# A grouped matrix product with residual: one x tile asked for ahead of a weight load, and the second half of the second weights prepared by three engines

## The chip, the cores and the metric

The kernel runs on 1 core of one Trainium2 chip. The metric is the device time in microseconds (us) of that core; the time of a kernel is the median of its runs. Within the core the engines named here are PE (TensorE, matmuls), PEld (its weight loads), DVE (VectorE), ACT (ScalarE), POOL (GpSimd) and SP (SyncE, which only issues transfers).

## The reference

There are 128 batches, each a 128 x 512 tile of x, and 32 classes, each with a 512 x 512 weight matrix and a bias row. Every batch has a class id from 0 to 30:

```python
selected_W = W[ids]                    # x: (128, 128, 512), W: (32, 512, 512)
selected_b = b[ids]
out = x + einsum('bti,bio->bto', x, selected_W) + selected_b[:, None, :]
```

Everything is float32. In the drawn ids class 0 has 6 batches, class 1 has 3, class 2 has 9 and class 3 has 4.

## The kernel before, in words

**The computation.** The residual is folded into the weights: 1 is added to the diagonal of every weight matrix, so out = x (W + I) + b. A product at float32 accuracy is made of three products of a faster format (fp32r): each operand is split into a high part (a rounded copy) and a low part (the operand less its high part). Per batch PE runs 4 row blocks x 3 pairs (high x with high W, high x with low W, low x with high W) = 12 matmuls of 128 x 128 by 128 x 512, all into one PSUM tile pA (four of them, used in turn). The batches are run in the order of their classes, so that the weights of each class are loaded once. The first instructions compute that order from the ids.

**The x tiles.** SP asks for tile i of x (function x_load, line 171; helper load, line 196) into one of 8 buffers xs. ACT (high, lines 308 to 317) writes the high part xh (line 314) and then a copy of x into PSUM, pT (line 317). DVE (low, line 372) writes the low part xl from pT and xh (line 375). For the first tile, and for the first weights, DVE subtracts from SBUF directly (lines 379 and 384). When a batch is done, DVE adds the bias to pA and writes os (line 411), and SP stores it (line 222). In DVE's program order low(i + 2) stands ahead of the addition of batch i. xh and xl have 4 buffers, pT has 3.

**The weights.** The first weights (class 0) are prepared in pieces by DVE (add_one, line 339: diagonal; low_w, line 384: low part) and ACT (high_w, line 306: high part). The second weights (class 1) come as two halves of 512 KB (w1_load, line 179, W1 = row blocks 0 and 1, then 2 and 3). POOL prepares each half alone: diagonal (line 255, tensor_tensor), high part wh (line 257, tensor_scalar), low part wl (line 259, tensor_tensor). Then it waits for a bias row, announces class 1 by s_w, asks for the next bias rows and the weights of class 3, and goes on with class 2 and all the others (lines 265 to 291), each with the same three steps on the whole matrix.

**The order around the change.** SP's queue is written out by hand (lines 205 to 217): x tile 1, first half of the second weights, x tiles 2 and 3, bias row 0, second half, x tile 4, the third weights, x tile 5, bias row 1, then the loop in which load(i + 6) stands ahead of the store of batch i. A batch on PE waits for its class's weights (s_w), for the addition of the batch four before (s_fin), for xh (s_xh) and, ahead of its low-x products, for xl (s_xl). Batches 1 to 5 run their high-x products first, later batches the low-x products first. Batch 0 is special: it is run from the pieces of the first weights (lines 477 and 488). The matmuls of all other batches are line 461.

Of the kernel before, what the change touches and what calls it, by code (L numbers as in the profile page):

```python
# [5 lines left out]
def cond_resid(nc, xt, ids, W, bias, out):  # L6
# [5 lines left out]
    f32 = mybir.dt.float32  # L12
# [3 lines left out]
    ALU = mybir.AluOpType  # L16
    ACT = mybir.ActivationFunctionType
    AX = mybir.AxisListType

    B, D = 128, 512  # L20
# [7 lines left out]
    NH = 4  # L28
# [3 lines left out]
    LA = 2  # L32
# [12 lines left out]
    with ExitStack() as ctx:  # L45
# [3 lines left out]
        def sem(name):  # L49
            return ctx.enter_context(nc.semaphore(name))  # L50
# [55 lines left out]
        s_b0 = [sem(f"s_b0{i}") for i in range(2)]  # L106
        s_bb = [sem(f"s_bb{i}") for i in range(C // NB)]
        s_wh = sem("s_wh")
        s_w = sem("s_w")
        s_raw = sem("s_raw")  # L110
        s_xb = sem("s_xb")
# [20 lines left out]
        def chunk(c, k0, k1):  # L132
            return slice(slot(c) + k0 * D, slot(c) + k1 * D)

        def raw(c, k0, k1):
            return wr[:, c % NR, k0 * D:k1 * D]

        def diagonal(c, k0, k1):

            t = wr[:, c % NR, k0 * D + k0 * 128:]  # L140
            return bass.AP(t.tensor, t.offset, [list(t.ap[0]), [D + 128, k1 - k0], [1, 128]])

        def ones_on(n):

            t = ident[:, :]
            return bass.AP(t.tensor, t.offset, [list(t.ap[0]), [0, n], [1, 128]])
# [27 lines left out]
        @block.sync  # L174
        def _(eng):
            eng.dma_start(idr[:, :], ids.rearrange("(a n) -> a n", a=1)).then_inc(s_id, 16)
            def w1_load(h):
                k0, k1 = W1[h]
                eng.dma_start(raw(1, k0, k1), stored(1, k0, k1)).then_inc(s_w1[h], 16)  # L179

            first = [eng.alloc_register(f"first{i}") for i in range(8)]
            lead = eng.alloc_register("lead")

            def sorted_first(i):
                return eng.snap(first[i], min_val=EXP, max_val=EXP + (C + 1) * B - 1) % B  # L185

            eng.wait_ge(s_t0, 1)
            eng.load(lead, best[:, :].bitcast(i32))  # L188
            x_load(eng, 0, bass.ds(eng.snap(lead, min_val=BITS, max_val=BITS + (C + 1) * B - 1) % B, 1))  # L189
            eng.dma_start(raw(0, 3, KT), stored(0, 3, KT)).then_inc(s_w0[2], 16)  # L190
            eng.wait_ge(s_t0, 2)
            eng.load(first, top[0:1, :])  # L192
            ahead = table(eng, "la", tbc, B, 0, B - 1)
            behind = table(eng, "st", tbc, B, 0, B - 1)

            def load(i):
                b = sorted_first(i) if i < 8 else ahead(i)
                if i == NX:
                    eng.wait_ge(s_xb, 2 * len(REST))
                    eng.wait_ge(s_mm, 2)  # L200
                elif i > NX:
                    eng.wait_ge(s_pt, i - NX)
                x_load(eng, i, bass.ds(b, 1))

            load(1)
            w1_load(0)
            load(2)
            load(3)
            bias_load(eng, 0, 1, s_b0[0])
            w1_load(1)  # L210
            load(4)
            eng.wait_ge(s_wd, KT)
            eng.wait_ge(s_raw, 1)
            eng.dma_start(wr[:, 0, :], stored(2, 0, KT)).then_inc(s_w2, 16)
            load(5)
            bias_load(eng, 1, 2, s_b0[1])
            eng.wait_ge(s_tab, 1)
            for i in range(B):
                if i + AHEAD < B:
                    load(i + AHEAD)  # L220
                b = behind(i)
                eng.dma_start(out[bass.ds(b, 1), :, :].rearrange("a t d -> (a t) d"), os[:, i % NO, :])\
                   ._wait_ge(s_fin, i + 1).then_inc(s_o[i % NO], 16)

        @block.gpsimd
        def _(eng):
            eng.iota(rev[:, :], [[1, 128]], base=C * B, channel_multiplier=0,
                     allow_small_or_imprecise_dtypes=True).then_inc(s_io, 1)
            eng.iota(iot[:, :], [[1, 128]], base=0, channel_multiplier=0,
                     allow_small_or_imprecise_dtypes=True).then_inc(s_io, 1)  # L230
            eng.memset(ident[:, :], 0.0).then_inc(s_cst, 1)
            eng.wait_ge(s_cst, 1)
            eng.affine_select(out=ident[:, :], in_=ident[:, :], compare_op=ALU.not_equal, fill=1.0,
                              base=0, pattern=[[-1, 128]], channel_multiplier=1).then_inc(s_cst, 1)
            eng.iota(dif[:, :], [[1, 128]], base=0, channel_multiplier=-1,
                     allow_small_or_imprecise_dtypes=True).then_inc(s_io, 1)
            eng.iota(num[:, 0:1], [[1, 1]], base=0, channel_multiplier=1,
                     allow_small_or_imprecise_dtypes=True).then_inc(s_io, 1)
            eng.iota(thr[:, :], [[B, C]], base=B, channel_multiplier=0,
                     allow_small_or_imprecise_dtypes=True).then_inc(s_io, 1)  # L240
            def load(c):
                eng.dma_start(wr[:, c % NR, :], stored(c, 0, KT)).then_inc(s_wr[c % NR], 16)  # L242
                if c % NB == 0:
                    bias_load(eng, c, c + NB, s_bb[c // NB])

            eng.sem_inc(s_w, 1)
            eng.wait_ge(s_cst, 2)
            done = table(eng, "dn", tn[2:3, :], C, 1, B + 1)
            eng.wait_ge(s_wd, KT)
            for h, (k0, k1) in enumerate(W1):  # L250
                half = raw(1, k0, k1)
                at = chunk(1, k0, k1)
                eye = diagonal(1, k0, k1)
                eng.wait_ge(s_w1[h], 16)
                eng.tensor_tensor(eye, eye, ones_on(k1 - k0), ALU.add).then_inc(s_ri, 1)  # L255
                eng.wait_ge(s_ri, 1 + h)
                eng.tensor_scalar(wh[:, at], half, 1.0, 1.0, ALU.mult, ALU.mult).then_inc(s_wh, 1)  # L257
                eng.wait_ge(s_wh, 1 + h)
                eng.tensor_tensor(wl[:, at], half, wh[:, at].bitcast(f32), ALU.subtract).then_inc(s_wp, 1)  # L259
            eng.wait_ge(s_wp, 2)  # L260
            eng.wait_ge(s_b0[1], 16)
            eng.sem_inc(s_w, 1)
            bias_load(eng, 2, NB, s_bb[0])
            load(3)
            for c in range(2, C):
                if c == 2:
                    eng.wait_ge(s_w2, 16)
                else:
                    eng.wait_ge(s_wr[c % NR], 16 * ((c - 1) // NR))
                eye = diagonal(c, 0, KT)  # L270
                eng.tensor_tensor(eye, eye, ones_on(KT), ALU.add).then_inc(s_ri, 1)  # L271
                at = chunk(c, 0, KT)
                if c == NW:
                    eng.wait_ge(s_tab, 3)
                if c >= NW:
                    n = done(c - NW)
                    eng.wait_ge(s_mm, n).then_inc(s_free, 1)
                eng.wait_ge(s_ri, 1 + c)
                eng.tensor_scalar(wh[:, at], wr[:, c % NR, :], 1.0, 1.0, ALU.mult, ALU.mult).then_inc(s_wh, 1)  # L279
                eng.wait_ge(s_wh, c + 1)  # L280
                if c % NB == 0:
                    eng.wait_ge(s_bb[c // NB], 16)
                eng.tensor_tensor(wl[:, at], wr[:, c % NR, :], wh[:, at].bitcast(f32),  # L283
                                  ALU.subtract).then_inc(s_wp if c == 2 else s_w, 1)
                if c == 2:
                    eng.wait_ge(s_wp, 3)
                    eng.wait_ge(s_bb[0], 16)
                    eng.sem_inc(s_w, 1)
                if c + NR < C:
                    eng.wait_ge(s_w, c + 1)  # L290
                    load(c + NR)

        @block.scalar
        def _(eng):
# [33 lines left out]
                high_0(ks, s_xb)  # L328
            for i in range(2, B):
                high(i)  # L330
        @block.vector
        def _(eng):
            n = [0]
# [66 lines left out]
            eng.tensor_scalar(tn[:, :], pS[0:3, B:B + C], 1.0, None, ALU.add).then_inc(s_tab, 1)  # L400
            eng.wait_ge(s_tab, 3)
            row = table(eng, "bo", tv[1:2, :], B, 0, (C - 1) * D)
            for i in range(B):
                if i + LA < B:
                    low(i + LA)
                at = row(i)
                if i == 0:
                    eng.wait_ge(s_b0[0], 16)
                if i >= NO:
                    eng.wait_ge(s_o[i % NO], 16 * (i // NO))  # L410
                eng.tensor_tensor(os[:, i % NO, :], pA[i % NA][:, :], bb[:, bass.ds(at, D)],  # L411
                                  ALU.add)._wait_ge(s_mm, i + 2).then_inc(s_fin, 1)
# [126 lines left out]
```

## Time and profile before

| | us |
|---|---|
| median of 3 runs | 359.7 |
| the 3 runs | 359.15, 359.70, 359.71 |
| the profiled execution, own time | 359.8 |
| its span in the trace | 358.5 |
| PE busy | 354.6 (99%) |
| DVE, ACT, POOL busy | 172.4, 146.8, 266.8 |

The span runs from the first to the last instruction that the profiler recorded; 1.3 us of the execution's own time lie around it. The granted TensorE clock is at full speed in all 40 slices of the page. Busy time says which engine has the most work; where a microsecond is lost is seen in the chain of waits and in the order of time.

### The profile page before, as it was taken

What the parts mean: (1) busy time and instruction counts of PE and PEld (TensorE: products, weight loads), DVE (VectorE), ACT (ScalarE), POOL (GpSimd) and SP (SyncE); (2) the same over time, 40 slices, a digit from 0 to 9 for tenths busy, and PEclk for the clock granted to TensorE, in tenths of its full rate; (3) what the DMA queues carried; (4) which work ended last, traced back from release to release, by engine and by line L of the source; (5) the groups of instructions that cost most, each with busy time, mean ns of one, the idle gap of its engine ahead of it and who ended that gap; (6) DMA issues with size and microseconds to landing.
All of it is one profiled execution on the core that took longest, in us unless ns stands there. A gap on an engine that the chain in (4) does not pass through costs nothing.

```text
span 358.5 us, 6658 instructions
## 1 busy us (share of the span) xinstructions
PE 354.6 (99%) x1554; PEld 290.2 (81%) x1554; DVE 172.4 (48%) x282; ACT 146.8 (41%) x263; POOL 266.8 (74%) x144
## 2 busy tenths in 40 slices
PE   9999999999999999999999999999999999999996
PEld 4788888888888888888888888888888888888885
DVE  7555355545544544554454454445445445544542
ACT  4564254434433443343443344344334253534420
POOL 1699999997747698799964999799979799935000
PEclk9999999999999999999999999999999999999999
DMA  7999998999886999889998899989998998856622
GB/s 225 375 311 406 413 348 314 324 375 358 280 313 242 354 317 309 295 297 359 338 306 291 283 388 314 341 290 371 317 331 272 358 379 298 327 207 194 191 105 100
DMA packets 43380, 109.49 MB, mean 305 GB/s; under 512 B 4817, under 2 KB 4818, under 8 KB 38610
## 3 DMA queue, kind: packets, MB, share of 16 engines
q1 hardware_dynamic: 37730, 70.01, 54.8%
q0 software_dynamic: 5328, 38.28, 30.8%
q10 hardware_dynamic: 288, 0.79, 0.6%
q8 instruction: 17, 0.28, 0.3%
q14 instruction: 17, 0.14, 0.1%
HBM read 75.50 MB, written 33.55 MB: 304 GB/s over the span
## 4 chain that ended last, share of the span: by engine, by line
PE 96%; DMA 2%; SPq 1%; DVE 0%; issue 0%; ACT 0%
PE pA L461 96%; DMA xs<-xt 2%; DMA idr<-ids 0%; SPq L171 0%; DVE os L411 0%; ACT xh L314 0%; SPq L192 0%; SPq L179 0%; SPq L190 0%; DVE top L354 0%; DVE key L351 0%; SPq L185 0%; SPq L188 0%; SPq L189 0%; DVE best L351 0%
## 5 line engine op out<-in xcount | busy, mean ns | idle before, releaser
L411 DVE TENSOR_TENSOR os<-pA,bb 128x512 f32<-128x512 f32 x128 | 88.5, 691 | 165.3 <-PE pA L461 164.7
L314 ACT ACTIVATE xh<-xs 128x512 fp32r<-128x512 f32 x126 | 79.7, 633 | 194.6 <-PE pA L461 108.4
L283 POOL TENSOR_TENSOR wl<-wr,wh 128x2048 fp32r<-128x2048 f32 x30 | 138.7, 4623 | 2.5
L461 PE MATMUL pA<-wh,xh 128*128 x508 | 135.9, 389 | 0.3 <-ACT xh L314 0.3
L461 PE MATMUL pA<-wl,xh 128*128 x508 | 135.8, 389 | 0.0
L461 PE MATMUL pA<-wh,xl 128*128 x508 | 135.6, 389 | 0.0
L461 PEld LDWEIGHTS pA<-wh,xh 128*128 128x128 f32 x508 | 95.3, 188 | 20.4 <-ACT xh L314 0.7
L461 PEld LDWEIGHTS pA<-wl,xh 128*128 128x128 f32 x508 | 95.4, 188 | 19.8
L461 PEld LDWEIGHTS pA<-wh,xl 128*128 128x128 f32 x508 | 95.4, 188 | 19.7
L375 DVE TENSOR_TENSOR xl<-pT,xh 128x512 fp32r<-128x512 f32 x127 | 86.6, 682 | 16.2 <-ACT pT L317 15.3
L279 POOL TENSOR_SCALAR wh<-wr 128x2048 fp32r<-128x2048 f32 x30 | 57.5, 1918 | 37.3 <-PE pA L461 35.4
L317 ACT ACTIVATE pT<-xs 128x512 f32<-128x512 f32 x126 | 73.5, 583 | 0.0
L271 POOL TENSOR_TENSOR wr<-wr,ident 128x512 f32<-128x512 f32 x30 | 39.2, 1307 | 1.0 <-DMA wr<-w 0.3
L242 POOL DMA_DIRECT2D wr<-w x29 | 17.1, 588 | 8.6 <-POOL wl L283 8.0
L255 POOL TENSOR_TENSOR wr<-wr,ident 128x256 f32<-128x256 f32 x2 | 1.5, 737 | 9.1 <-DMA wr<-w 9.1
L418 PE MATMUL pA<-const-bfloat16-1.0 128*128 128x512 bf16 (+1 forms) x16 | 5.1, 486 | 0.8 <-PEq L532 0.8
L150 POOL DMA_DIRECT2D bb<-bias x8 | 4.5, 559 | 0.7 <-POOL wl L259 0.7
L259 POOL TENSOR_TENSOR wl<-wr,wh 128x1024 fp32r<-128x1024 f32 x2 | 4.8, 2410 | 0.2
L418 PEld LDWEIGHTS pA<-const-bfloat16-1.0 128*128 128x128 bf16 x16 | 1.7, 134 | 2.7 <-issue 2.4
L306 ACT ACTIVATE wh<-wr 128x512 fp32r<-128x512 f32 x4 | 2.3, 618 | 2.1 <-DVE wr L339 2.1
L384 DVE TENSOR_TENSOR wl<-wr,wh 128x512 fp32r<-128x512 f32 x4 | 2.7, 689 | 0.2
L257 POOL TENSOR_SCALAR wh<-wr 128x1024 fp32r<-128x1024 f32 x2 | 2.1, 1050 | 0.2
(51 smaller groups left out, 19.4 us busy)
## 6 DMA issues: line engine op xcount, KB each, us to landing
xs<-xt SPq DMA_DIRECT2D x128, 256.0 KB, 5.8
out<-os SPq DMA_DIRECT2D x128, 256.0 KB, 5.2
wr<-w POOLq DMA_DIRECT2D x29, 1024.0 KB, 7.7
bb<-bias POOLq DMA_DIRECT2D x7, 1024.0 KB, 10.4
wr<-w SPq DMA_DIRECT2D x2, 512.0 KB, 6.8
wr<-w SPq DMA_DIRECT2D x1, 1024.0 KB, 8.6
wr<-w ACTq DMA_DIRECT2D x1, 512.0 KB, 3.3
bb<-bias SPq DMA_DIRECT2D x2, 256.0 KB, 7.8
```

The costliest lines, as they stand in the source:

```text
L150: eng.dma_start(bb[:, at].rearrange("p (c d) -> p c d", c=j1 - j0), bias[j0:j1, :].rearrange("(a c) d -> a c d", a=1).to_broadcast([128, j ...
L242: eng.dma_start(wr[:, c % NR, :], stored(c, 0, KT)).then_inc(s_wr[c % NR], 16)
L259: eng.tensor_tensor(wl[:, at], half, wh[:, at].bitcast(f32), ALU.subtract).then_inc(s_wp, 1)
L271: eng.tensor_tensor(eye, eye, ones_on(KT), ALU.add).then_inc(s_ri, 1)
L279: eng.tensor_scalar(wh[:, at], wr[:, c % NR, :], 1.0, 1.0, ALU.mult, ALU.mult).then_inc(s_wh, 1)
L283: eng.tensor_tensor(wl[:, at], wr[:, c % NR, :], wh[:, at].bitcast(f32), ALU.subtract).then_inc(s_wp if c == 2 else s_w, 1)
L314: eng.activation(xh[:, i % NH, :, :], xs[:, i % NX, :, :], ACT.Copy).then_inc(s_xh, 1)
L317: eng.activation(pT[i % NT][:, :, :], xs[:, i % NX, :, :], ACT.Copy).then_inc(s_pt, 1)
L375: eng.tensor_tensor(xl[:, i % NH, :, :], pT[i % NT][:, :, :], xh[:, i % NH, :, :].bitcast(f32), ALU.subtract).then_inc(s_xl, 1)
L411: eng.tensor_tensor(os[:, i % NO, :], pA[i % NA][:, :], bb[:, bass.ds(at, D)], ALU.add)._wait_ge(s_mm, i + 2).then_inc(s_fin, 1)
L418: eng.matmul(pA[0][:, 0:w], fill[:, 0:128], fill[:, 0:w], start=True, stop=True)
L461: mm = eng.matmul(pA[i % NA][:, :], xp[:, i % NH, k, :], wp[:, bass.ds(at + k * D, D)], start=(n == 0), stop=(n == 3 * KT - 1))
```

## The change

Three things. On SP's queue the request for x tile 2 stands ahead of the first half of the second weights. For the second half of the second weights DVE adds the diagonal (signal s_rb), ACT writes the high part (signal s_hb) and POOL writes only the low part. ACT's instruction stands behind high(3), and waits there for s_rb. On DVE the low parts of x tiles 2 and 3 are written first, then DVE waits for the half to land and adds the diagonal, and only then comes the loop with the additions of the bias (in it the low parts from tile 4 on). In POOL's loop over the later classes two waited counts are one smaller, since POOL itself counts one diagonal and one high part fewer.

```diff
-            w1_load(0)
             load(2)
+            w1_load(0)
             load(3)
             bias_load(eng, 0, 1, s_b0[0])
             w1_load(1)
...
-            for h, (k0, k1) in enumerate(W1):
-                half = raw(1, k0, k1)
-                at = chunk(1, k0, k1)
-                eye = diagonal(1, k0, k1)
-                eng.wait_ge(s_w1[h], 16)
-                eng.tensor_tensor(eye, eye, ones_on(k1 - k0), ALU.add).then_inc(s_ri, 1)
-                eng.wait_ge(s_ri, 1 + h)
-                eng.tensor_scalar(wh[:, at], half, 1.0, 1.0, ALU.mult, ALU.mult).then_inc(s_wh, 1)
-                eng.wait_ge(s_wh, 1 + h)
-                eng.tensor_tensor(wl[:, at], half, wh[:, at].bitcast(f32), ALU.subtract).then_inc(s_wp, 1)
+            eye = diagonal(1, *W1[0])
+            eng.wait_ge(s_w1[0], 16)
+            eng.tensor_tensor(eye, eye, ones_on(W1[0][1]), ALU.add).then_inc(s_ri, 1)
+            eng.wait_ge(s_ri, 1)
+            eng.tensor_scalar(wh[:, chunk(1, *W1[0])], raw(1, *W1[0]), 1.0, 1.0, ALU.mult, ALU.mult).then_inc(s_wh, 1)
+            eng.wait_ge(s_wh, 1)
+            for h in range(2):
+                at = chunk(1, *W1[h])
+                if h == 1:
+                    eng.wait_ge(s_hb, 1)
+                eng.tensor_tensor(wl[:, at], raw(1, *W1[h]), wh[:, at].bitcast(f32), ALU.subtract).then_inc(s_wp, 1)
...
-                eng.wait_ge(s_ri, 1 + c)
+                eng.wait_ge(s_ri, c)
...
-                eng.wait_ge(s_wh, c + 1)
+                eng.wait_ge(s_wh, c)
...
             for i in range(2, B):
                 high(i)
+                if i == NH - 1:
+                    eng.wait_ge(s_rb, 1)
+                    eng.activation(wh[:, chunk(1, *W1[1])], raw(1, *W1[1]), ACT.Copy).then_inc(s_hb, 1)
...
+            for i in range(LA, NH):
+                low(i)
+            eye = diagonal(1, *W1[1])
+            eng.wait_ge(s_w1[1], 16)
+            eng.tensor_tensor(eye, eye, ones_on(2), ALU.add).then_inc(s_rb, 1)
             for i in range(B):
-                if i + LA < B:
+                if NH <= i + LA < B:
                     low(i + LA)
```

## Rows read from the trace of the kernel before

**Rows 1.** The page: the chain that ended last, by line; and one group.

```profile
PE pA L461 96%; DMA xs<-xt 2%; DMA idr<-ids 0%; SPq L171 0%; DVE os L411 0%; ACT xh L314 0%; SPq L192 0%; SPq L179 0%; SPq L190 0%; DVE top L354 0%; DVE key L351 0%; SPq L185 0%; SPq L188 0%; SPq L189 0%; DVE best L351 0%
...
L375 DVE TENSOR_TENSOR xl<-pT,xh 128x512 fp32r<-128x512 f32 x127 | 86.6, 682 | 16.2 <-ACT pT L317 15.3
```

**Rows 2.** Chain that ended last, in order of time: start us, us, what.

```profile
5.79 6.20 DMA xs<-xt
...
12.01 0.64 ACT xh L314
...
12.69 343.03 PE pA L461 x1512
```

**Rows 3.** Timeline of PE: start us, us, instruction [idle before <-releaser].

```profile
9.50 1.07 PE L461 MATMUL pA<-wh,xh 128*128 x4
...
15.55 1.07 PE L461 MATMUL pA<-wh,xh 128*128 x4
...
20.99 1.07 PE L461 MATMUL pA<-wh,xh 128*128 x4
...
354.64 1.07 PE L461 MATMUL pA<-wh,xh 128*128 x4
```

**Rows 4.** Timeline of SP's queue, same columns; L171 x tiles, L179 second weights.

```profile
5.13 0.43 SPq L179 DMA_DIRECT2D wr<-w  x1
5.79 0.90 SPq L171 DMA_DIRECT2D xs<-xt  x2
...
7.21 1.18 SPq L179 DMA_DIRECT2D wr<-w  x1
...
17.48 0.34 SPq L171 DMA_DIRECT2D xs<-xt  x1
...
21.71 0.34 SPq L171 DMA_DIRECT2D xs<-xt  x1
```

**Rows 5.** DMA issues at 4.74, 5.13, 7.21: count, KB, us from issue to landing.

```profile
xs<-xt SPq DMA_DIRECT2D x1, 256.0 KB, 4.1
...
wr<-w SPq DMA_DIRECT2D x1, 512.0 KB, 6.2
...
wr<-w SPq DMA_DIRECT2D x1, 512.0 KB, 7.5
```

**Rows 6.** Groups by shape, 0 to 20 us: count | busy us, mean ns | idle before.

```profile
L339 DVE TENSOR_TENSOR wr<-wr,ident 128x256 f32<-128x256 f32 x1 | 0.4, 419 | 0.0
...
L306 ACT ACTIVATE wh<-wr 128x512 fp32r<-128x512 f32 x4 | 2.3, 618 | 2.1 <-DVE wr L339 2.1
...
L302 ACT ACTIVATE xh<-xs 128x128 fp32r<-128x128 f32 x1 | 0.3, 293 | 0.0
```

**Rows 7.** Timeline of ACT, columns as in 3: high parts of x tiles 4, 5, 10.

```profile
15.37 0.63 ACT L314 ACTIVATE xh<-xs 128x512 fp32r<-128x512 f32 x1 [1.20 <-DMA xs<-xt]
...
18.58 0.63 ACT L314 ACTIVATE xh<-xs 128x512 fp32r<-128x512 f32 x1 [2.08 <-DMA xs<-xt]
...
30.43 0.63 ACT L314 ACTIVATE xh<-xs 128x512 fp32r<-128x512 f32 x1 [5.24 <-DMA xs<-xt]
```

**Rows 8.** Timeline of POOL, columns as in 3.

```profile
11.48 0.74 POOL L255 TENSOR_TENSOR wr<-wr,ident 128x256 f32<-128x256 f32 x1 [9.14 <-DMA wr<-w]
...
13.44 2.41 POOL L259 TENSOR_TENSOR wl<-wr,wh 128x1024 fp32r<-128x1024 f32 x1
...
20.88 0.74 POOL L150 DMA_DIRECT2D bb<-bias  x1 [0.70 <-POOL wl L259]
...
25.60 4.62 POOL L283 TENSOR_TENSOR wl<-wr,wh 128x2048 fp32r<-128x2048 f32 x1
```

**Rows 9.** Timeline of DVE, columns as in 3: the last SBUF-only subtraction, the first two additions.

```profile
10.81 0.28 DVE L379 TENSOR_TENSOR xl<-xs,xh 128x128 fp32r<-128x128 f32 x1
...
14.35 0.69 DVE L411 TENSOR_TENSOR os<-pA,bb 128x512 f32<-128x512 f32 x1 [0.40 <-issue]
...
15.56 0.68 DVE L411 TENSOR_TENSOR os<-pA,bb 128x512 f32<-128x512 f32 x1
```

More of the change, by code:

```diff
@@ L108, in cond_resid @@
         s_wh = sem("s_wh")
+        s_rb = sem("s_rb")
+        s_hb = sem("s_hb")
         s_w = sem("s_w")
@@ L205, in _ @@
             load(1)
+            load(2)
             w1_load(0)
-            load(2)
             load(3)
```

## Prediction

> **What bounds the kernel now.** I read the page's chain first: 96% of the span is the matmul line 461, and the next piece is a transfer of x with 2% [rows 1]. The chain in order of time says which transfer: x tile 2, asked for at 5.79 and landed 6.20 later, at 11.99, then the high part of that tile, and from 12.69 on nothing but 1512 matmuls [rows 2]. So the time is a start, one hole, and an unbroken run. The timeline of PE gives the hole and the pace. From 15.55 (batch 3) to 354.64 (the ninth matmul of batch 127) lie 124 batches and 8 matmuls: 339.09 / (124 + 8/12) = 2.720 us a batch. Batch 1 starts at 9.50, so batch 3 would start at 9.50 + 2 x 2.72 = 14.94 if nothing were late; it starts at 15.55 [rows 3]. **0.61 us** is all that the early x tile can bring: 0.47 that batch 2 starts late (12.69 against 12.22) and 0.14 lost while the stopped pipeline fills again (12.69 to 15.55 is 2.86) [rows 2, 3]. Anything late afterwards costs its delay and 0.14 more, once, at whichever batch it hits. I therefore check each due time of the first ten batches.
>
> A difference of 0.2%, 0.72 us, is about what a measurement of this kernel tells from no change. Even the full 0.61 stays inside it.
>
> **Part 1: x tile 2 ahead of the half.** Its request moves from 5.79 to about 5.3 (the register work of some 0.2 between 5.56 and 5.79 moves with it) and 512 KB no longer stand ahead of it. x tile 1 landed at 4.74 + 4.1 = 8.84, the first half at 5.13 + 6.2 = 11.33, x tile 2 at 11.99 [rows 2, 4, 5]: 256 KB behind the half took 0.66. Tile 2 should land between 8.84 + 0.66 = 9.5 and, if it waits as the half did, 11.33. Due is 12.22 less 0.64 for the high part and 0.05 for signals, 11.5. Both ends are in time, so the hole at batch 2 goes: **-0.61**. The half takes tile 2's place in the order and lands at about 11.99 (bounds 11.33 and 11.99; the bytes of both are the same, so I take the upper one). POOL starts on it 0.5 later than the 11.48 of before. All that stands behind the two on SP keeps its place and its bytes: tile 3, bias row 0, and the second half, which lands at 7.21 + 7.5 = **14.71** [rows 4, 5].
>
> **Part 2: the second half's steps.** The diagonal on DVE is 128 x 256, 0.42 alone [rows 6]. The high part on ACT is 128 x 1024; from 0.293 at 128 columns to 0.618 at 512 a further 128 columns cost 0.108, so 0.618 + 4 x 0.108 = 1.05 [rows 6]. Both must be over before ACT starts the high part of x tile 4 (0.63), which batch 4 needs first of all. That tile itself had landed at 15.3 and ACT was idle before it [rows 7]. On DVE the low parts of tiles 2 and 3 only move ahead of an addition that had time; they are over by about 14.6, before the half lands. Batch 4 is due at 9.50 + 3 x 2.72 = 17.66.
>
> *If the diagonal runs at once:* 14.74 to 15.16, ACT's weights to 16.25, high part of tile 4 to 16.92. Batch 4 can start at 17.66 with 0.5 to spare (the weight load of PE wants it some 0.2 earlier). Cost nothing; the cover is ACT's idle time of 1.20 ahead of tile 4 [rows 7], and if it were gone, each tenth would show at batch 4 after the first half microsecond.
>
> *If the diagonal is held up by POOL:* at 14.74 POOL is inside its low part of the first half. Started at 12.03, POOL's chain takes 13.44 + 2.41 - 11.48 = 4.37 as before [rows 8] and ends at 16.40; the low part alone occupies it from 13.99. The trace of before has no row of the disputed kind. DVE instructions that read both operands from SBUF, lines 339, 379 and 384, all end by 11.1, and POOL's first instruction on weights starts at 11.48 [rows 8, 9]; every later DVE instruction has one operand in PSUM. So the diagonal's cost is bounded by 0.42 (alone) and by 16.40 - 14.74 + 0.42 = 2.08 (after POOL's instruction); a gain is excluded, as its own time is the least. I take the upper end. The row that it is nearest to in time, place and operands is POOL's low part of 2.41, which reads the same tile wr while it runs; the rows that say 0.42 are of a time when POOL was idle.
>
> The Trainium skill says the same in "SBUF — State Buffer", section "SBUF: two separate sides": VectorE with two SBUF inputs and a GpSimd instruction that reads SBUF exclude each other by a lock on a shared pair of ports, and the second one waits for the whole of the first. It speaks against this change; no run here shows it yet. By that rule the sum is the upper one, without it the lower.
>
> The sum with the hold-up: diagonal 16.43 to 16.85; weights on ACT 16.89 to 17.94; high part of tile 4, with 0.04 for the change of instruction, to 18.62; batch 4 starts at 18.67 and batch 5, with the refill, at 18.67 + 2.86 = **21.53**. Before, batch 5 started at 20.99 [rows 3]. The difference is **+0.54**. It does not depend on when batch 2 started: what part 1 gains (0.61) is waited away at batch 4. Against its own time the execution gives 359.8 + 0.54 = 360.34; the median of the runs stands 0.1 below that execution, so 360.24; with a tenth for the signals' jitter between four engines I give **360.3**.
>
> **Part 3: what is queued behind.** ACT's wait also holds tile 5, landed about 18.55 [rows 7]: its high part ends about 19.8, due 21.4. DVE's wait holds the additions of batches 0 and 1: they move from 14.35 and 15.56 [rows 9] to about 17.25 and 17.95 (the 0.40 ahead of the first taken along). Batch 4 needs the first, ended 17.94, at 18.67: in time. Low part of tile 4: after the copy to PSUM at 19.2, done 19.9, due 18.67 + 0.14 + 8/12 of 2.72 = 20.6. SP's queue is in program order, so the stores of batches 0 and 1 and the requests for tiles 7 and 8 behind them move too, tile 8 from 17.48 [rows 4] to about 19.9. Tile 8 is due (low-x products first, so after high part, copy and low part, 0.63, about as much again and 0.68, with signals, some 1.95, and 0.2 for the weight load) at 21.53 + 3 x 2.72 - 2.15 = 27.5, 7.6 from issue.
>
> POOL loses a diagonal and a high part and waits for ACT instead: its second low part runs 18.0 to 20.4 against an end of 20.2 before, so class 1 is announced about 21.1 (20.88 before [rows 8]), due with batch 6 at 24.3. Class 2 was ready at 30.22 [rows 8] and was due with batch 9 at 15.55 + 6 x 2.72 = 31.9; now some 30.5 against 32.4. The other classes keep their distances. One less POOL chain is worth nothing to a kernel that PE bounds.
>
> **Rivals.**
>
> *No hold-up.* The diagonal runs beside POOL in 0.42, nothing is late at batch 4, the 0.61 is kept: 359.8 - 0.6 = 359.2 for the execution, 359.1 for the median. For it: POOL and DVE ran side by side with the 127 low parts of line 375 at an even 0.68 [rows 1], though each with a PSUM operand. POOL would be done at about 18.9 in this case, its next transfers go out earlier, and no due time is worse. 0.27.
>
> *Late x tiles, the slower side.* DVE's long wait pushes the stores and requests on SP. Tile 10, issued at 21.71, landed only by 30.43, 8.7 later, beside the bias rows that POOL asked for at 20.88 and the weights behind them [rows 4, 7, 8]. If tile 8, issued at 19.9, fares the same, it lands at 28.6, 1.1 after its due time; with the refill of 0.14 that is 1.2 over the plain case: 361.5. It decides where tile 8 takes over 7.6. Against it: it is asked for a microsecond before those transfers, and less stands ahead of it on SP. 0.10.
>
> *Tile 2 comes no earlier.* The swap does nothing; the hold-up still sets batch 4, so the time is again 360.3, and without the hold-up 359.7. 0.08, and it hardly moves the numbers.
>
> **How the numbers follow.** Hold-up with its plain price: 0.55, 360.3, its own range 359.9 to 360.8, since POOL's end moves by up to 0.6 downward with the half's landing and by a few tenths upward with signals. No hold-up 0.27 at 359.1, late tiles 0.10 at 361.5, tile 2 unmoved 0.08. The bound upward is 360.42: about four in ten of the plain case lie above it, 0.22, with the late tiles 0.10 makes 0.32. The bound downward is 358.98: a bit under half of the no-hold-up case, 0.12. The rest, 0.56, is within. The range must reach to the no-hold-up case: 359.0 to 361.1 leaves out the late tiles and half of what lies below.
>
> **What would show it.** The hole at 12.4 in PE's timeline is gone and x tile 2 has landed by 11. In the hold-up case DVE's new 128 x 256 addition begins or ends with the end of POOL's 128 x 1024 subtraction, near 16.4, ACT's 128 x 1024 copy of about 1.07 starts near 16.9, and PE waits for ACT's line of high parts with about 1 us at batch 4, which starts near 18.7; batch 5 starts near 21.5. If instead the addition ends near 15.2 and batch 5 starts near 20.4, the hold-up is wrong. An idle PE after 24 us would mean the late tiles.

## The result, and the profile after

| | before | changed |
|---|---|---|
| median | 359.32 (22 runs) | 360.35 (22 runs) |
| lowest, highest | 359.11, 360.71 | 359.33, 364.34 |
| runs over 360 | 2 of 22 | 14 of 22 |
| profiled execution, own time | 359.8 | 364.34 |
| its span | 358.5 | 363.0 |

The ratio is 1.0036, 95% interval 1.0022 to 1.0051: slower, by more than the 0.2% that I called no change. The median is the forecast one (360.3) and lies in its range, but the median before, with 22 runs instead of 3, is 359.32 and not 359.7. So the change costs about 1.0 us in the median (1.3 us in the mean, which the ratio follows) where I had forecast 0.6 over 359.7, and what it costs varies from run to run, which I had not forecast. The lowest runs are almost as good as the lowest of before; the upper half is spread over 4 us.

The profiled execution of the changed kernel is the slowest of the 22. Its chain of waits, in order of time (start us, us, what), shows where:

```profile
10.93 16.33 PE pA L472 x72
27.27 0.02 issue
27.29 0.70 DVE os L422
...
28.01 0.35 SPq L224
...
28.61 14.68 DMA xs<-xt
...
43.85 0.59 ACT pT L320
...
44.53 0.70 DVE xl L381
45.23 0.28 issue
45.51 314.70 PE pA L472 x1380
```

Against [rows 2] the piece of x that the chain passes through is another one. Batches 1 to 6 run (72 matmuls), DVE adds the bias of batch 6, SP stores it and only then asks for x tile 13, which takes 14.68 us to land. Tile 13 was asked for at 28.61; before, at 27.95, and it took 7.2. PE's timeline, the matmuls that answer to [rows 3] and those around the hole:

```profile
10.77 1.07 PE L472 MATMUL pA<-wh,xh 128*128 x4
...
13.49 1.07 PE L472 MATMUL pA<-wh,xh 128*128 x4
...
16.21 1.07 PE L472 MATMUL pA<-wh,xh 128*128 x4
...
18.93 1.07 PE L472 MATMUL pA<-wh,xh 128*128 x4
...
21.65 1.07 PE L472 MATMUL pA<-wh,xh 128*128 x4
...
42.65 1.07 PE L472 MATMUL pA<-wh,xh 128*128 x4
45.51 1.19 PE L472 MATMUL pA<-wh,xl 128*128 x4 [1.80 <-DVE xl L381]
46.54 1.75 PE L472 MATMUL pA<-wl,xh 128*128 x4
48.09 1.91 PE L472 MATMUL pA<-wh,xh 128*128 x4
49.80 1.24 PE L472 MATMUL pA<-wh,xl 128*128 x4
```

Batches 1 to 5 start at 10.77, 13.49, 16.21, 18.93 and 21.65, each 2.72 after the one before. The hole at batch 2 is gone, and batch 4 is not late. Batch 13 should start at 43.56 and starts at 45.51. After that the fours of matmuls take 1.75 and 1.91 instead of 1.07. The windows say why (window, length, PE busy, PEld, DVE, ACT, POOL, granted clock, DMA share, GB/s):

```profile
44.00:45.00 1.00, 0.00 (x0) 0.00 (x0) 0.47 (x1) 0.85 (x2) 0.92 (x2) 1.00 1.13 457
45.00:46.00 1.00, 0.49 (x2) 0.47 (x3) 1.00 (x3) 0.70 (x2) 1.00 (x1) 1.00 0.95 399
46.00:47.00 1.00, 1.00 (x6) 0.79 (x5) 1.00 (x2) 0.53 (x1) 1.00 (x1) 0.85 0.85 352
47.00:48.00 1.00, 1.00 (x4) 0.81 (x3) 0.40 (x2) 0.59 (x2) 1.00 (x1) 0.50 0.98 328
...
50.00:51.00 1.00, 1.00 (x5) 0.82 (x5) 0.89 (x2) 0.85 (x3) 0.97 (x2) 0.94 1.18 283
```

PE did nothing for 1.8 us, and from 46.7 to about 50.1 the granted clock is 0.50, the lower of the two levels (1.2 GHz); nowhere else is it below full in this stretch. So the late tile costs 1.95 of waiting and then 1.73 of slow matmuls and refill (batch 13 takes 4.28, batch 14 2.89, instead of 2.72 each). The books of this execution against the one of before: start of batch 1 +1.27 (10.77 against 9.50), hole at batch 2 -0.61, batch 10 +0.13, batch 13 late +1.95, slow clock +1.73, together +4.47 of the 4.5 us between the spans. The late start is 0.4 us of a late transfer of the ids and, for the rest, a slow batch 0: its first two matmuls of high parts take 1.82 here and 1.02 before. In all other executions batch 1 starts between 9.30 and 9.92. What slowed batch 0 stays open.

The disputed instruction in this execution, DVE's diagonal and POOL's first low part:

```profile
15.24 0.43 DVE L413 TENSOR_TENSOR wr<-wr,ident 128x256 f32<-128x256 f32 x1 [1.29 <-DMA wr<-w]
```

```profile
12.89 2.40 POOL L262 TENSOR_TENSOR wl<-wr,wh 128x1024 fp32r<-128x1024 f32 x1
```

POOL's instruction ends at 15.29, where I had 16.40, and the second half lands at 15.2, where I had 14.71. They meet almost exactly, and the diagonal takes 0.43. One execution can't say whether there is a hold-up, and one at the edge of 22 runs can't say where the median goes. Both needed runs.

### The profile page after: what moved, and what is told of

Same layout as the page of the kernel before. It is cut to its first block, busy times and chain, and to the rows that moved or that the text cites. A ratio compares the mean times of both kernels' runs of the same rounds, so it can differ in the third digit from the quotient of the medians.

```text
span 363.0 us, 6658 instructions
## 1 busy us (share of the span) xinstructions
PE 357.2 (98%) x1554; PEld 291.7 (80%) x1554; DVE 173.0 (48%) x283; ACT 147.7 (41%) x264; POOL 265.0 (73%) x142
## 4 chain that ended last, share of the span: by engine, by line
PE 93%; DMA 5%; DVE 1%; issue 0%; ACT 0%; SPq 0%; DVEq 0%
PE pA L472 91%; DMA xs<-xt 4%; PE pA L429 1%; PE pA L499 1%; PE pA L488 0%; DMA idr<-ids 0%; DVE os L422 0%; DVE xl L381 0%; ACT pT L320 0%; SPq L224 0%; DVE top L360 0%; DVE key L357 0%; DVE idb L362 0%; PE pS L444 0%; PE pS L436 0%
## 5 line engine op out<-in xcount | busy, mean ns | idle before, releaser
L381 DVE TENSOR_TENSOR xl<-pT,xh 128x512 fp32r<-128x512 f32 x127 | 86.6, 682 | 15.8 <-ACT pT L320 15.2
L499 PE MATMUL pA<-wh,xh 128*128 128x512 f32 x3 | 2.2, 806 | 0.0
```

Source lines behind the costliest of these rows:

```text
L381: eng.tensor_tensor(xl[:, i % NH, :, :], pT[i % NT][:, :, :], xh[:, i % NH, :, :].bitcast(f32), ALU.subtract).then_inc(s_xl, 1)
L499: return eng.matmul(pA[0][:, :], xp[:, 0, k, :], wp[:, chunk(0, k, k + 1)], start=False, stop=stop)
```

## The experiments

Three groups of four, each with its own runs of the kernel before (29, 35 and 28 of them, medians 359.39, 359.45 and 359.46). The first group ran on one chip, the other two on another. The interval behind a ratio is the 95% one. In the profiles the lost time is the start of batch 127 less the start of batch 1 less 126 x 2.72; some 0.1 at batch 2 is in nearly all of them.

### The change again, its two parts alone, and the disputed instruction alone

**The changed kernel once more.** No edit.

> The changed kernel, a second look, since the first profiled execution (364.3) lies far above its median (360.35). Theory H (the diagonal is held up by POOL): batch 4 starts about 1 us late in any execution, ratio to before about 1.0015. Theory X (late x tiles): batches 1 to 7 follow each other without a hole, batch 3 starts some 0.6 earlier than before, and the loss comes at batches 12 to 14, whose x tile is landed 11 us or more after it was asked for, beside POOL's 2 MB of weights and bias rows; ratio between 0.998 (tiles in time) and 1.01 (a tile late), differing from run to run.

Measured: ratio 1.0013 (1.0002 to 1.0024), 5 of 12 runs over 360. The profiled execution (359.68) has this diagonal:

```profile
15.11 0.78 DVE L413 TENSOR_TENSOR wr<-wr,ident 128x256 f32<-128x256 f32 x1 [1.41 <-DMA wr<-w]
```

```profile
13.20 2.40 POOL L262 TENSOR_TENSOR wl<-wr,wh 128x1024 fp32r<-128x1024 f32 x1
```

The diagonal begins at 15.11, POOL's subtraction ends at 15.60, and the diagonal ends 0.29 after it, at 15.89: 0.78 instead of 0.42. There is a hold-up, and here it lengthens the row by 0.36. PE doesn't feel it: batch 4 starts at 17.57, in time, where theory H had it 1 us late. Batch 5 is 0.31 late, but for its x tile:

```profile
19.91 0.63 ACT L317 ACTIVATE xh<-xs 128x512 fp32r<-128x512 f32 x1 [1.92 <-DMA xs<-xt]
```

Lost in all 0.64. Theory X isn't seen in this execution: tiles 9 and 13 landed in time.

**Only the order on SP.**

```diff
-            w1_load(0)
             load(2)
+            w1_load(0)
```

> Only x tile 2 is asked for ahead of the half; the second weights are prepared by POOL alone. Both theories: the hole at batch 2 goes, 0.6 us or 0.17% faster than before (ratio 0.998 to 0.999). Theory X adds: POOL is no earlier, PE and with it SP's requests are 0.6 earlier, so no x tile is late and the runs scatter no more than those of before.

Measured: ratio 1.0001 (0.9992 to 1.0010), 2 of 11 runs over 360. The hole is gone, and nothing is gained. The execution profiled (359.25) loses 0.15 in all. An unchanged order loses as little at batch 2 when its tile comes in time: in the executions of the four other kernels below that keep the old order (only the second half's steps, the disputed instruction alone, only DVE's wait, only late requests) x tile 2 landed at 10.9, 10.8, 11.9 and 10.2, against 12.0 in [rows 2], and none of them loses more than 0.14 there. The one with 11.9 had luck: its batch 1 started 0.4 late (9.92), so the tile was still in time. The hole that I read belongs to one execution; the landing behind it scatters over 1.8 us. The lowest times of this kernel (359.14) and of before (359.12) are the same floor.

**Only the second half's steps**, with the old order on SP.

> Only the second half's steps are given to DVE, ACT and POOL; the order of the transfers is that of before. The hole at batch 2 stays. Theory H: besides it batch 4 starts late where the first half lands late enough, ratio 1.001 to 1.003. Theory X: POOL's 2 MB go out 0.5 to 1.5 us earlier while the requests for x tiles 12 to 14 go out as before or later, so a tile is late in a good part of the runs: ratio 1.002 to 1.006, with runs scattered by over 1 us upward.

Measured: ratio 1.0021 (1.0006 to 1.0037), 7 of 12 over 360, up to 362.17. The profiled execution (360.48) shows two late tiles, 10 and 13. ACT waiting for tiles 9, 10 and 13:

```profile
28.67 0.63 ACT L317 ACTIVATE xh<-xs 128x512 fp32r<-128x512 f32 x1 [4.63 <-DMA xs<-xt]
...
32.25 0.63 ACT L317 ACTIVATE xh<-xs 128x512 fp32r<-128x512 f32 x1 [2.46 <-DMA xs<-xt]
...
41.04 0.63 ACT L317 ACTIVATE xh<-xs 128x512 fp32r<-128x512 f32 x1 [4.89 <-DMA xs<-xt]
```

SP's requests of tiles 7, 8, 9 and 13, and POOL's bias rows and weights:

```profile
16.87 0.34 SPq L173 DMA_DIRECT2D xs<-xt  x1
...
19.66 0.34 SPq L173 DMA_DIRECT2D xs<-xt  x1
...
20.79 0.34 SPq L173 DMA_DIRECT2D xs<-xt  x1
...
27.26 0.34 SPq L173 DMA_DIRECT2D xs<-xt  x1
```

```profile
20.37 0.74 POOL L152 DMA_DIRECT2D bb<-bias  x1 [1.77 <-DMA bb<-bias]
21.11 0.56 POOL L244 DMA_DIRECT2D wr<-w  x1
...
30.32 0.58 POOL L244 DMA_DIRECT2D wr<-w  x1 [0.62 <-POOLq L291]
30.90 0.55 POOL L152 DMA_DIRECT2D bb<-bias  x1
```

Before, tiles 7, 8 and 9 were asked for at 15.66, 17.48 and 18.61 (the second in [rows 4]); now at 16.87, 19.66 and 20.79. POOL asks for its 1.5 MB at 20.37 and 21.11 (20.88 [rows 8] and 21.62 before). Tile 9 went out 2.3 ahead of them before and landed after 5.4; now it goes out 0.4 behind the first and lands after 7.9, and tile 10 behind it at 32.2 instead of the 30.43 of [rows 7], too late for its batch. Between 35.0 and 41.0 no x tile lands at all, and tile 13 is the one that falls in: 13.8 us. Before, tile 13 landed at 35.1 and tile 14, with more time to spare, was the first behind the pause, at 41.4. Its own request is 0.7 earlier than before (27.26 against 27.95); it stands behind tiles 10 to 12, and these land 0.9 to 1.8 later than before. Here the cost is 1.43: 0.56 at batch 10, 0.44 at batch 13, 0.33 for the refills and the 0.10 of batch 2. Tiles 8 and 9 were asked for 2.2 later than before, POOL's transfers 0.5 earlier, so most of the change in their order is on SP's side. Theory X holds in this execution; what it put down to POOL belongs mostly to the requests.

**The disputed instruction alone.**

```diff
+                if 30 <= i < 50:
+                    if i > 30:
+                        eng.wait_ge(s_pr, i - 30)
+                    eng.tensor_tensor(probe[:, :], bb[:, 0:256], bb[:, 256:512], ALU.add).then_inc(s_pr, 1)
```

> The kernel before, with 20 extra DVE additions of 128 x 256 in batches 30 to 49 that read both operands from SBUF and write a scratch tile (the disputed cost by itself). POOL works on weights in most of that stretch. Theory H: those that begin beside a POOL instruction take or wait until it ends, durations or starts late by up to 4.6 us, many rows far over 0.42 or an idle time ahead of them. If there is no hold-up: all 20 take 0.41 to 0.44, directly behind the addition of the bias. The time is that of before in either case unless a hold-up of 4 us reaches PE.

Measured: a single run of 360.9, lost 1.76. The extra line's group (duration ns min/median/max, first and last start), and DVE and POOL in 9 us of it:

```profile
L418 DVE TENSOR_TENSOR probe<-bb x20: 410/1278/3644, 92.0 to 147.3; 128x256 f32<-128x256 f32 x20
```

```profile
94.22 0.68 DVE L413 TENSOR_TENSOR os<-pA,bb 128x512 f32<-128x512 f32 x1
94.82 3.64 DVE L418 TENSOR_TENSOR probe<-bb 128x256 f32<-128x256 f32 x1
...
98.98 0.68 DVE L413 TENSOR_TENSOR os<-pA,bb 128x512 f32<-128x512 f32 x1
99.58 1.10 DVE L418 TENSOR_TENSOR probe<-bb 128x256 f32<-128x256 f32 x1
```

```profile
93.51 4.66 POOL L285 TENSOR_TENSOR wl<-wr,wh 128x2048 fp32r<-128x2048 f32 x1
98.47 0.58 POOL L244 DMA_DIRECT2D wr<-w  x1 [0.30 <-POOL wl L285]
99.08 1.30 POOL L273 TENSOR_TENSOR wr<-wr,ident 128x512 f32<-128x512 f32 x1
```

This is how a hold-up looks in a trace: no idle time, but a long row. The addition begins at 94.82, POOL's instruction ends at 98.17, and the addition ends at 98.46, 0.29 behind it. The next, at 99.58, ends 0.30 after POOL's instruction of 99.08 to 100.38. The additions with a PSUM operand between them, beside the same POOL instructions, take 0.68 as ever. Of the 20 extra additions 14 lie beside a POOL instruction, and each of them ends 0.27 to 0.30 behind it (one began 0.03 ahead of POOL's and was held up too); the other 6 take 0.41. Theory H is shown as a mechanism: up to 3.64 for an instruction of 0.41. The Trainium skill's rule ("SBUF — State Buffer", "SBUF: two separate sides"), that the second of the two waits for the whole of the first, agrees with these rows.

### Which wait makes the tiles late

**Only DVE's wait**, on the kernel before.

```diff
+            for i in range(LA, NH):
+                low(i)
+            eng.wait_ge(s_w1[1], 16)
             for i in range(B):
-                if i + LA < B:
+                if NH <= i + LA < B:
                     low(i + LA)
```

> The kernel before with one thing of the change: DVE writes the low parts of tiles 2 and 3 and then waits for the second half to land before the first addition of the bias; no step of the weights is moved and POOL works as before. Theory L (late requests: DVE's wait pushes the stores of batches 0 and 1 and the requests of x tiles 7 to 9 behind them by 1.5 to 2 us, and a tile that so falls behind POOL's bias rows lands 4 to 6 us later): requests of tiles 7, 8, 9 near 17, 19.5, 20.7 instead of 15.7, 17.5, 18.6, holes at batches 9 or 13 in some runs, ratio 1.001 to 1.003 as with the split. Theory P (it is POOL's burst, which the split sends 0.5 us earlier): ratio 1.000, no holes after batch 3.

Measured: ratio 1.0015 (0.9996 to 1.0034), 3 of 12 over 360, one of them 363.43. The requests of tiles 7, 8 and 9 do go out late, at 17.3, 19.1 and 20.2, but in the profiled execution all land in time (lost 0.16). The ratio is nearer to L than to P, and not enough to decide: the interval reaches from nothing to the whole effect.

**The changed kernel with the diagonal behind the first addition of the bias.**

```diff
-            eye = diagonal(1, *W1[1])
-            eng.wait_ge(s_w1[1], 16)
-            eng.tensor_tensor(eye, eye, ones_on(2), ALU.add).then_inc(s_rb, 1)
...
+                if i == 0:
+                    eye = diagonal(1, *W1[1])
+                    eng.wait_ge(s_w1[1], 16)
+                    eng.tensor_tensor(eye, eye, ones_on(2), ALU.add).then_inc(s_rb, 1)
```

> The changed kernel with DVE's diagonal of the second half behind the addition of batch 0 instead of ahead of it. Theory L: the first store goes out near 15 and the request of tile 7 near 15.7 again, tiles 9 and 13 land before the stretches in which none lands, no hole after batch 3; ratio to before 0.999 to 1.000, 0.1% to 0.2% below the changed kernel. Theory P: POOL is as early as in the changed kernel, so the holes stay, ratio 1.001 to 1.003.

Measured: ratio 1.0004 (0.9995 to 1.0012), 2 of 12 over 360, the highest 360.17. Tile 7 goes out at 15.7 again, and the scatter upward is gone. That fits L, but it doesn't decide. Tiles 8, 9 and 13 go out at 18.7, 20.2 and 27.8, where the three profiled executions of the changed kernel have 19.1 to 20.0, 20.2 to 21.2 and 27.3 to 28.6, so only tiles 7 and 8 are clearly earlier; and POOL asks at 21.2 where it asked at 20.0 to 21.2 there and at 20.9 before, so for this execution theory P expects no loss either. The group has no runs of the changed kernel to compare with: the ratio lies below that of the third group, on the same chip (1.0028, below), and its interval overlaps that of the first (1.0013).

What is left in the profiled execution (lost 0.66) lies at batches 4 to 7. Here the held-up diagonal reaches PE:

```profile
15.31 0.73 DVE L424 TENSOR_TENSOR wr<-wr,ident 128x256 f32<-128x256 f32 x1 [0.26 <-DMA wr<-w]
16.08 1.06 ACT L336 ACTIVATE wh<-wr 128x1024 fp32r<-128x1024 f32 x1 [2.91 <-DVE wr L424]
```

POOL's subtraction ends at 15.77 and the diagonal 0.27 behind it; ACT's high part of tile 4 stands behind its copy of the weights, and batch 4 starts at 17.71, 0.11 late. Batch 5 is 0.20 late for tile 5, which landed at 19.9.

**The first half late, so that POOL's work lies over the landing of the second.**

```diff
             load(2)
-            w1_load(0)
             load(3)
             bias_load(eng, 0, 1, s_b0[0])
+            w1_load(0)
             w1_load(1)
```

> The changed kernel with the first half asked for only behind tile 3 and bias row 0, so that POOL starts on it near 12 and its low part runs to about 16.4, over the landing of the second half near 14.8. Theory H (DVE's addition with two SBUF operands waits for POOL's instruction): the diagonal's row lasts 1.5 to 2 us and ends near 16.7, batch 4 starts near 18.5 instead of 17.6, batch 5 near 21.4. Without a hold-up: the diagonal takes 0.42 and batch 4 starts by 17.7. By theory L some runs have later holes besides, ratio 1.003 to 1.006.

**The same with the ones in PSUM.**

```diff
+        ident2 = ones_on(2)
+        ones_ps = pS[:, 256:512].rearrange("p (a c) -> p a c", a=2)
...
                 if i == NH - 1:
+                    eng.wait_ge(s_cst, 2)
+                    eng.wait_ge(s_tab, 3)
+                    eng.activation(ones_ps, ident2, ACT.Copy).then_inc(s_pi, 1)
                     eng.wait_ge(s_rb, 1)
...
+            eng.wait_ge(s_pi, 1)
-            eng.tensor_tensor(eye, eye, ones_on(2), ALU.add).then_inc(s_rb, 1)
+            eng.tensor_tensor(eye, eye, ones_ps, ALU.add).then_inc(s_rb, 1)
```

> As the late half, but the ones that DVE adds lie in PSUM (ACT copies the identity there after the high part of tile 3), so that the diagonal has one SBUF operand. Theory H: it takes 0.4 to 0.5 beside POOL's instruction, ends near 15.3, batch 4 is late by at most 0.3; about 0.8 us less than the late half. Without a hold-up there would be no difference to the late half.

Measured: 1.0009 (0.9999 to 1.0019) and 1.0007 (0.9995 to 1.0019); the times don't tell the two apart. The rows do. The late half, POOL and DVE:

```profile
14.12 1.05 POOL L256 TENSOR_SCALAR wh<-wr 128x1024 fp32r<-128x1024 f32 x1
14.43 1.01 DVE L413 TENSOR_TENSOR wr<-wr,ident 128x256 f32<-128x256 f32 x1 [1.89 <-DMA wr<-w]
```

With the ones in PSUM:

```profile
15.35 1.06 POOL L260 TENSOR_SCALAR wh<-wr 128x1024 fp32r<-128x1024 f32 x1
15.65 0.42 DVE L421 TENSOR_TENSOR wr<-wr,pS 128x256 f32<-128x256 f32 x1 [2.33 <-DMA wr<-w]
```

Both begin 0.3 inside POOL's instruction, which here has a single SBUF input. With two SBUF operands the addition ends 0.27 after it, at 15.44; with one it takes 0.42 and ends while POOL still works. But I missed the aim with both: the first half landed at 13.1 and 14.4, later than the 12 that I had counted on, so the addition met the short instruction and slipped in ahead of the 2.4 us one. The price of the long hold-up at batch 4, some 1 us in my sum, was therefore never run in place.

### More of the suspected cost, and less

**The changed kernel, third time.** No edit.

> The changed kernel once more, as the yardstick of this group on its chip: ratio to before 1.001 to 1.004, about half of the runs over 360 and some over 361, as in the two groups before it.

Measured: ratio 1.0028 (1.0014 to 1.0041), 10 of 12 over 360. The three sets of runs of this kernel give 1.0036, 1.0013 and 1.0028; together 29 of 46 runs lie over 360. The profiled execution (359.18) is the best of its twelve and loses 0.12: the same program can run without a hole, with its diagonal held up by 0.23.

**The changed kernel, seven tiles ahead.**

```diff
-    AHEAD = 6
+    AHEAD = 7
...
             bias_load(eng, 1, 2, s_b0[1])
+            load(6)
             eng.wait_ge(s_tab, 1)
```

> The changed kernel with SP asking for x tiles seven ahead instead of six (tile 7 ahead of the first store, each later one a batch of 2.7 us earlier). Theory L (the loss is late x tiles, behind requests that DVE's wait pushes back): tiles 9 and 13 land in time in every run, no holes at batches 8 to 16, no run over 361, ratio to before 0.999 to 1.0005, at least 0.1% below the changed kernel. If the loss lay in the hold-up or in ACT's wait at batch 4: no difference to the changed kernel.

Measured: ratio 1.0008 (0.9999 to 1.0017), 2 of 11 over 360, the highest 360.32, on the chip where the changed kernel gave 1.0028 (1.0014 to 1.0041), 10 of 12 and 361.43. Tiles 9 and 13 are asked for at 19.8 and 25.7 and land at 24.0 and 34.1, 7.5 and 8.3 ahead of their batches. DVE's wait, ACT's wait and the three engines' steps are all as in the changed kernel; only the requests are earlier, and most of the loss is gone. The loss is that of late x tiles, as L has it, and not the hold-up or ACT's wait. Whether DVE's wait or POOL's lead makes them late, this run can't tell: earlier requests help against both.

**The order on SP and seven tiles ahead**, on the kernel before.

> The candidate for the best: only x tile 2 ahead of the first half, and requests seven ahead; nothing moved off POOL. Theory L: PE runs without a hole from batch 1 on in every run, 359.1 to 359.4, ratio 0.9985 to 0.9995. Rival: the extra request ahead of the first store (256 KB at 11 us) delays tiles 5 and 6 or a weight load, ratio 1.000 to 1.002.

Measured: ratio 1.0005 (0.9996 to 1.0014), 2 of 11 over 360. No gain; if anything the rival's side of the expectation. Its profiled execution (360.23) lost 1.19 at batches 4 to 6, where PE waited for tile 5:

```profile
20.49 0.63 ACT L315 ACTIVATE xh<-xs 128x512 fp32r<-128x512 f32 x1 [3.57 <-DMA xs<-xt]
...
21.17 1.20 PE L462 MATMUL pA<-wh,xh 128*128 x4 [0.73 <-ACT xh L315]
```

Tile 5 was asked for at 9.9 to 10.3 in every kernel. With the old order it landed at 18.0 to 18.7 in four executions and at 20.6 in one, with the new order at 18.7 to 20.5 in nine (19.3 or later in eight of them). So the new order may give back at batch 5 what it gains at batch 2; no run was made to show it.

**Only late requests, and more of them**, on the kernel before.

```diff
                 if i + AHEAD < B:
                     load(i + AHEAD)
+                if i == 0:
+                    eng.wait_ge(s_x[5], 16)
```

> The kernel before with the suspected cost alone and larger: SP waits for x tile 5 (near 18.6) ahead of the first store, which pushes the requests of tiles 7, 8 and 9 back by about 3.5, 3 and 2.5 us; DVE, ACT and POOL are as before. Theory L: tiles 9 to 13 land late, holes at batches 9 to 14 in most runs, ratio 1.002 to 1.008 with a wide scatter. If late requests cost nothing: ratio 1.000.

Measured: 364.94, ratio 1.0148 (1.0115 to 1.0180), 6 runs of 363.1 to 367.17: more than expected. Tile 5 landed at 20.6 (and made batch 5 1.0 late by itself), so the first store waited till 21.4 and tiles 7, 8 and 9 went out at 21.95, 23.70 and 24.83. That is 6.2 to 6.3 later than before, about twice the push that I had meant, and that of the changed kernel is 1.6 to 2.6. Tile 8, behind POOL's transfers, landed at 31.5:

```profile
31.53 0.63 ACT L316 ACTIVATE xh<-xs 128x512 fp32r<-128x512 f32 x1 [5.49 <-DMA xs<-xt]
...
33.74 2.07 PE L463 MATMUL pA<-wh,xl 128*128 x4 [3.62 <-DVE xl L377]
```

The microsecond behind the hole (columns as in the windows of the result):

```profile
34.00:35.00 1.00, 1.00 (x3) 0.82 (x4) 1.00 (x3) 1.00 (x2) 0.91 (x2) 0.50 1.05 406
```

A wait on a queue that computes nothing, ahead of a store that nobody waits for, costs 5.5 us in the median: batch 8 is 3.9 late and then runs at the lower clock (granted 0.50). Late requests alone suffice for a loss of this kind. What a push of 2 us costs by itself, this run doesn't say.

## Why the prediction was right or wrong

**Part 1, x tile 2 brings 0.61: mis-sized.** The tile landed at 9.0 to 9.5 with the new order, at the early end that I had, and the hole vanished. But the step "0.61 us is all that the early x tile can bring" took one execution's hole for the kernel's. The order alone measured a ratio of 1.0001 (0.9992 to 1.0010), no gain, where 0.61 us would be 0.9983. A difference of 0.55 between three runs of the same kernel (359.15 and 359.70) was in front of me, and was the size of that hole.

**The half takes tile 2's place and lands at 11.99: wrong.** It landed at 10.5 to 11.2 in the seven executions with the new order, and at 9.5 to 11.3 with the old one. I took the upper bound because the bytes ahead were the same; but the same bytes land up to 1.8 us apart in different executions. On this number hung the price of the next step.

**Part 2, the diagonal is held up by POOL until 16.40: mechanism right, price wrong.** The disputed instruction alone and the pair with and without the ones in PSUM show the hold-up. POOL's subtraction ended at 15.29, 15.60 and 15.21 in the three executions of the changed kernel, 0.8 to 1.2 earlier than in my sum, so the hold-up was 0.01, 0.36 and 0.23 instead of 1.66. Batch 4 started in time in all three. The +0.54 at batch 5 did not occur in any of them: the 0.31 of the second execution is x tile 5's. The term for ACT's 128 x 1024 copy (1.05) measured 1.06.

**Part 3, what is queued behind.** The requests moved as I had worked out: tile 8 to 19.1 to 20.0 (forecast 19.9). I checked tile 8, found 7.6 us enough, and it was: it landed within 4.7. I then stopped. The tiles that failed are 10, behind POOL's first transfers and a tile 9 that used to be ahead of them, and 13, at the edge of POOL's next. "I check each due time of the first ten batches" was the wrong limit, since a delay on SP's queue stays there until PE's pace swallows it.

**The rivals.** "Late x tiles" is what happened, at 13 and 10 rather than 8, in two profiled executions and, by the runs with seven tiles ahead, in most of the slower runs: 0.10 was too little for it, and its price, 1.2, was close to the usual one (most runs of the upper half lie 1.0 to 2.0 above the lowest times) but missed the lower clock, which turned 1.95 into 3.7. "No hold-up" nearly described the best quarter of the runs (359.2 to 359.8), without the gain. So the number was right by luck, through errors that cancel: a base that was 0.4 too high (359.7 from three runs, 359.32 from 22), a hold-up at batch 4 that isn't there in that size (0.54), and late tiles, about 1 us in the median, that were not in the sum. What I held most likely, no change at 0.56, is not what was measured.

**What stays open.** That the loss is late x tiles is shown by the two profiled executions with a late tile and by the edit that makes only the requests earlier, against the changed kernel on the same chip (1.0008 and 1.0028, intervals that overlap by 0.0003; 2 of 11 and 10 of 12 runs over 360). That late requests alone can do it is shown by the large copy of the cost. That it is DVE's wait, more than POOL's half microsecond of lead, that makes them late is argued from the request times: DVE's wait alone gave no clear answer, and POOL's lead alone was not run. Nor does it take effect each time: in the third set's execution tile 9 went out 0.2 behind POOL's request (20.21 against 20.03) and landed after 4.3, in time; in the two with a late tile it went out 0.4 and 0.7 behind it and landed after 7.9 and 8.9. Why no x tile lands between about 35 and 41, beside POOL's transfers, was not tried; before, in that stretch, the 16 DMA engines are busy (shares of 0.93 to 1.09) and move 371 to 449 GB/s. I didn't run the changed kernel with a long hold-up in place.

No version was found that beats the kernel before.

## What to carry to other kernels

One profiled execution shows one draw: before a hole in it is priced as a gain, compare its size with the scatter of the runs, since a hole as large as that scatter may not be there in the median. When a wait is added, follow the queue behind it for transfers, not only the engine, and on to the last one that the delay still reaches: a request that slips behind another queue's megabytes can pay several times its own delay (tile 13: asked for 0.7 later, landed 8.2 later). A VectorE instruction with two SBUF operands and a GpSimd instruction that reads SBUF should be planned one after the other, or one operand of VectorE's moved to PSUM.

## What was unexpected about the hardware

- A VectorE addition with two SBUF operands that starts beside a GpSimd instruction with at least 0.25 us to go ends 0.27 to 0.30 us after it, however long that is (3.64 instead of 0.41 at most), also where the GpSimd instruction has one SBUF input. Begun 0.05 and 0.12 us ahead of the end, it takes 0.43 and 0.42. The row is long, and no idle time is shown.
- In every profiled execution there is a pause of 4.1 to 6.7 us, beginning between 33 and 38, in which no x tile lands although the DMA engines are busy (in the kernel before a share of 0.93 or more in each microsecond of it): 35.1 to 41.4 before, 37.1 to 43.3 in the slowest run of the changed kernel.
- An idle PE of 1.8 us was followed, 1.2 us after it took up work, by some 3.4 us at a granted clock of 0.50; one of 3.6 us, in the run with the waiting store, by 3.4 us at 0.50, at once. Idle times of 0.3 to 0.9 us were followed by none.
